# Two recurrent chains merged into one: both batches in one 512-column product, the line and the bias written into PSUM before it

## The reference

```
def _conv1d(x, w, b):
    y = jax.lax.conv_general_dilated(x, w, window_strides=(1,), padding=[(2, 2)], dimension_numbers=('NCH', 'OIH', 'NCH'))
    return y + b[None, :, None]
...
def step(w, b):

    def f(carry, inp):
        nxt = inp + _conv1d(carry, w, b)
        return (nxt, nxt)
    return f
...
_, d_rest = jax.lax.scan(step(down_w, down_b), d0, xs[1:])
...
_, u_rest = jax.lax.scan(step(down_w, down_b), u0, seq)
...
_, r_rest = jax.lax.scan(step(right_w, right_b), r0, ws[1:])
...
_, l_rest = jax.lax.scan(step(left_w, left_b), l0, R[Ww - 2::-1])
...
x = x + _L1_conv_ref(_gn(x), L1_conv_down_w, L1_conv_down_b, L1_conv_right_w, L1_conv_right_b, L1_conv_left_w, L1_conv_left_b)
```

## Time and profile before

| | |
|---|---|
| device time, median of 3 runs | 10,235.59 us (10,228.61 to 10,245.71) |
| span of the profiled execution | 10,244.7 us |
| recurrences, first to last product's start | 5097.5 to 9501.8 us |
| TensorE busy | 9248.3 us, 90% |
| VectorE busy | 7669.6 us, 75% |
| ScalarE busy | 6283.6 us, 61% |
| GpSimd busy | 2991.7 us, 29% |

### The profile page before, as it was taken

One profiled execution on the slowest core, in us unless ns is written; L12 is line 12 of the kernel. 1 busy time (PEld: TensorE's weight loads), 2 busy tenths in 40 slices (PEclk: granted clock), 3 DMA queues, 4 the chain that ended last, 5 costly groups with the idle time before them and its releaser, 6 DMA issues. The chain is left out here.

```text
span 10244.7 us, 212155 instructions
## 1 busy us (share of the span) xinstructions
PE 9248.3 (90%) x72264; PEld 8910.2 (87%) x72264; DVE 7669.6 (75%) x15539; ACT 6283.6 (61%) x11050; POOL 2991.7 (29%) x4335
## 2 busy tenths in 40 slices
PE   3999999999999999999899999999999999999100
PEld 3999999999999997777699999999999999999100
DVE  8888888777777775666677777777899987777323
ACT  3777777777777775444466668999633346666000
POOL 0000000000000000000166666666666666666000
PEclk9999999999999999999899999999999999999555
DMA  8888887666666666999889896777766657777999
GB/s 269 168 170 168 168 170 143 131 129 133 136 131 135 135 131 150 291 278 293 235 191 195 203 195 191 219 210 217 210 205 217 211 184 200 196 203 188 370 433 401
DMA packets 770603, 2101.31 MB, mean 205 GB/s; under 512 B 58976, under 2 KB 633728, under 8 KB 674256
## 3 DMA queue, kind: packets, MB, share of 16 engines
q1 hardware_dynamic: 629824, 1744.21, 66.6%
q0 software_dynamic: 34304, 151.01, 5.7%
q10 hardware_dynamic: 106368, 204.76, 5.6%
HBM read 1344.55 MB, written 754.97 MB: 205 GB/s over the span
## 5 line engine op out<-in xcount | busy, mean ns | idle before, releaser
L1542 ACT CAST hi<-rough 112x256 fp32r<-112x256 f32 x4096 | 1666.2, 407 | 1414.4 <-DVE rough L1455 1362.8
L1375 PE MATMUL scan_ps<-hi,scan_high 112*112 112x256 f32 x12264 | 2122.7, 282 | 30.7 <-ACT hi L1542 30.7
L1455 DVE SCALAR_TENSOR_TENSOR rough<-scan_ps,scan_bias,lines 112x256 f32<-112x256 f32 x4086 | 2136.4, 523 | 18.4 <-issue 14.0
L1386 PE MATMUL scan_ps_low<-lo,scan_high 112*112 112x256 f32 x12264 | 2136.1, 283 | 0.9 <-POOL lo L1487 0.7
L1381 PE MATMUL scan_ps_low<-hi,scan_low 112*112 112x256 f32 x12264 | 2123.9, 282 | 0.0
L463 PE MATMUL conv_ps<-tap_low,x_high 128*128 128x432 f32 (+2 forms) x6144 | 1905.4, 310 | 0.0
L463 PE MATMUL conv_ps<-tap_high,x_low 128*128 128x432 f32 (+2 forms) x6144 | 1904.0, 310 | 0.0
L463 PE MATMUL conv_ps<-tap_high,x_high 128*128 128x432 f32 (+2 forms) x6144 | 1882.0, 306 | 11.7 <-DVE x_edge L659 7.3
L1375 PEld LDWEIGHTS scan_ps<-hi,scan_high 112*112 112x112 f32 x12264 | 1695.0, 176 | 32.0 <-ACT hi L1542 31.5
L1386 PEld LDWEIGHTS scan_ps_low<-lo,scan_high 112*112 112x112 f32 x12264 | 1685.7, 176 | 6.3 <-POOL lo L1487 2.1
L1381 PEld LDWEIGHTS scan_ps_low<-hi,scan_low 112*112 112x112 f32 x12264 | 1684.1, 176 | 0.0
(11 more groups left out here) (142 smaller groups left out, 11625.5 us busy)
## 6 DMA issues: line engine op xcount, KB each, us to landing
raw<-x SPq DMA_DIRECT2D x764, 256.0 KB, 5.0
d_rows<-lines SPq DMA_DIRECT2D x32, 3584.0 KB, 30.4
u_cols<-lines SPq DMA_DIRECT2D x64, 1792.0 KB, 13.3
r_cols<-lines SPq DMA_DIRECT2D x32, 3584.0 KB, 24.3
lines<-u_cols SPq DMA_DIRECT2D x31, 3584.0 KB, 16.5
lines<-r_cols SPq DMA_DIRECT2D x30, 3584.0 KB, 16.6
lines<-d_rows SPq DMA_DIRECT2D x30, 3360.0 KB, 15.7
v_blocks<-xs ACTq DMA_DIRECT2D x128, 768.0 KB, 4.5
```

The source lines that it names most:

```text
L1375: last = nc.tensor.matmul(ps[:, b, 0:LP], high[:, shift], hi[:, b, (k - 1) % 2, shift:shift + LP], start=shift == 0, stop=shift == 2)
L1386: last = nc.tensor.matmul(ps_low[:, b, 0:LP], high[:, shift], lo[:, b, shift:shift + LP], start=False, stop=shift == 2)
L1455: nc.vector.scalar_tensor_tensor(rough[:, b, k % 2], ps[:, b, 0:LP], bias, line(way, s, k % T, b, kept), ALU.add, ALU.add).then_inc(rough_ ...
L1542: nc.scalar.copy(hi[:, b, k % 2, 1:LP + 1], rough[:, b, k % 2]).then_inc(hi_ready[b], 1)
```

## The change

Both batches of a line now share every instruction: products are 512 columns wide (two batches of 256), with one set of semaphores. PSUM holds four slots of 512 columns (`SLOTS`), and all nine products of a line add up in one of them. Before the first of them, VectorE writes the input line and the bias into the slot (`seed`); in "down" it writes scale and shift of the normalising in the same pass, one instruction for each batch, and ScalarE's normalising is gone. ScalarE reads `hi` from the slot after the three high products; when the six low products are in too, VectorE subtracts `hi` from the slot, which gives `lo`; the state is `hi` + `lo`, by GpSimd. `hi` has four buffers and `lo` two. ScalarE's turning copies run two lines later (`LAG`). SyncE's loads and stores wait on `seeded` and `state_done` in place of the per-batch semaphores. At the start four products set up the slots.

```diff
+    LAG = 2
+    AHEAD = 2
+    HIS, LOS, SLOTS = 4, 2, 4
...
-            return ctx.enter_context(nc.psum_tensor(name, [PP, B, 512], F32))
+            return ctx.enter_context(nc.psum_tensor(name, [PP, SLOTS, B, LP], F32))
...
-        rough = sb("rough", [PP, B, 2, LP])
-        hi = sb("hi", [PP, B, 2, LP + 2], F32R)
-        lo = sb("lo", [PP, B, LP + 2], F32R)
+        hi = sb("hi", [PP, HIS, B, LP + 2], F32R)
+        lo = sb("lo", [PP, LOS, B, LP + 2], F32R)
...
+        def slot_free(engine, way, g, k, kept):
+
+            if not (way == "down" and kept and k < SLOTS):
+                engine.wait_ge(lo_ready, states0(way) + T * g + k - SLOTS + 1)
+
+        def high_free(engine, way, g, k, first):
+
+            if not (way == "down" and first and k < HIS):
+                engine.wait_ge(state_done, states0(way) + T * g + k - HIS + 1)
...
-                def steps(way, g, start):
-                    high, low = w_hi[:, TAPS_OF[way]], w_lo[:, TAPS_OF[way]]
-                    done = states0(way) + T * g
-                    for k in range(start, 2 * T):
-                        for b in range(B):
-
-                            pe.wait_ge(hi_ready[b], done + k)
-                            for shift in range(3):
-                                last = nc.tensor.matmul(ps[:, b, 0:LP], high[:, shift], hi[:, b, (k - 1) % 2, shift:shift + LP],
-                                                        start=shift == 0, stop=shift == 2)
-                            last.then_inc(conv_done[b], 1)
-
-                            pe.wait_ge(state_done[b], done + k)
-                            for shift in range(3):
-                                nc.tensor.matmul(ps_low[:, b, 0:LP], low[:, shift], hi[:, b, (k - 1) % 2, shift:shift + LP],
-                                                 start=shift == 0, stop=False)
-
-                            pe.wait_ge(lo_ready[b], done + k)
-                            for shift in range(3):
-                                last = nc.tensor.matmul(ps_low[:, b, 0:LP], high[:, shift], lo[:, b, shift:shift + LP],
-                                                        start=False, stop=shift == 2)
-                            last.then_inc(low_done[b], 1)
+                def slot(k):
+                    return ps[:, k % SLOTS]
+
+                def high_products(way, g, k):
+
+                    pe.wait_ge(seeded[way], T * g + k + 1)
+                    pe.wait_ge(hi_ready, states0(way) + T * g + k)
+                    for shift in range(3):
+                        last = nc.tensor.matmul(slot(k), w_hi[:, TAPS_OF[way], shift], hi[:, (k - 1) % HIS, :, shift:shift + LP],
+                                                start=False, stop=False, skip_group_check=True)
+                    last.then_inc(conv_done, 1)
+
+                def low_products(way, g, k):
+
+                    pe.wait_ge(hi_ready, states0(way) + T * g + k + 1)
+                    for shift in range(3):
+                        nc.tensor.matmul(slot(k), w_lo[:, TAPS_OF[way], shift], hi[:, (k - 1) % HIS, :, shift:shift + LP],
+                                         start=False, stop=False, skip_group_check=True)
+
+                    pe.wait_ge(lo_ready, states0(way) + T * g + k)
+                    for shift in range(3):
+                        last = nc.tensor.matmul(slot(k), w_hi[:, TAPS_OF[way], shift], lo[:, (k - 1) % LOS, :, shift:shift + LP],
+                                                start=False, stop=shift == 2, skip_group_check=True)
+                    last.then_inc(low_done, 1)
+
+                def steps(way, g, first=False, last=False):
+                    for k in range(2 * T):
+                        if not (last and k == 2 * T - 1):
+                            high_products(way, g, k + 1)
+                        if not (first and k == 0):
+                            low_products(way, g, k)
 
...
+                for j in range(SLOTS):
+
+                    nc.tensor.matmul(slot(j), w_hi[:, 0, 0], hi[:, 0, :, 0:LP], start=True, stop=False, skip_group_check=True
+                                     ).then_inc(slots_set, 1)
                 for way in WAYS:
-                    steps(way, 0, 1)
-                    with pe.Fori(1, G // 2) as i:
-                        steps(way, 2 * i, 0)
+                    steps(way, 0, first=True)
+                    with pe.Fori(1, G // 2 - 1) as i:
+                        steps(way, 2 * i)
+                    steps(way, G - 2, last=True)
...
+                def seed(way, g, s, k, kept=False, bare=False):
+
+                    arrived(v, way, g, s, k % T, kept)
+                    slot_free(v, way, g - s, k, kept)
+                    to, of = ps[:, k % SLOTS], line(way, s, k % T, kept)
                     if way == "down":
-                        if k % 2 == 0:
-                            v.wait_ge(normed, T * g + k + 2)
-                    elif kept and KEPT[way][s]:
-                        if way == "up" and s == 1 and k == T - 1:
-                            v.wait_ge(skipped_in, 16)
-                    elif k == 0:
-                        v.wait_ge(loaded[way][s], landed(way, g, s))
-
+                        shift = gn1_bias if bare else down_shift
+                        for b in range(B):
+                            ins = nc.vector.tensor_scalar(to[:, b], of[:, b], gn1_scale[:, b:b + 1], shift[:, b:b + 1], ALU.mult, ALU.add)
+                    elif bare:
+                        ins = nc.vector.tensor_copy(to, of)
+                    else:
+                        ins = nc.vector.tensor_scalar(to, of, b_sb[:, TAPS_OF[way]:TAPS_OF[way] + 1], None, ALU.add)
+                    ins.then_inc(seeded[way], 1)
+
+                def steps(way, g, first=False, last=False):
+                    for k in range(2 * T):
+                        done = states0(way) + T * g + k
+                        v.wait_ge(hi_ready, done + 1)
+                        if not (first and k == 0):
+                            v.wait_ge(low_done, convs0(way) + T * g + k)
+                        if not (way == "down" and first and k < LOS):
+                            v.wait_ge(state_done, done - LOS + 1)
+                        nc.vector.tensor_tensor(low_of(k), ps[:, k % SLOTS], high_of(k), ALU.subtract).then_inc(lo_ready, 1)
+                        ahead = k + AHEAD
+                        if ahead < 2 * T:
+                            seed(way, g + ahead // T, ahead // T, ahead, first)
+                        elif not last:
+                            seed(way, g + ahead // T, ahead // T - 2, ahead - 2 * T)
+
...
-                            v.wait_ge(conv_done[b], convs + k)
-                            nc.vector.scalar_tensor_tensor(rough[:, b, k % 2], ps[:, b, 0:LP], bias, line(way, s, k % T, b, kept),
-                                                           ALU.add, ALU.add).then_inc(rough_ready[b], 1)
-
-                            v.wait_ge(low_done[b], convs + k)
-                            v.wait_ge(rough_ready[b], done + k + 1)
-                            nc.vector.tensor_tensor(state(way, s, k, b), ps_low[:, b, 0:LP], rough[:, b, k % 2],
-                                                    ALU.add).then_inc(state_done[b], 1)
...
+                        pool.wait_ge(hi_ready, states0(way) + T * g + k + 1)
+                        pool.wait_ge(lo_ready, states0(way) + T * g + k + 1)
+                        nc.gpsimd.tensor_tensor(state(way, s, k), high_of(k), low_of(k), ALU.add).then_inc(state_done, 1)
...
-                            nc.scalar.copy(hi[:, b, k % 2, 1:LP + 1], rough[:, b, k % 2]).then_inc(hi_ready[b], 1)
...
-                        if way == "down":
-                            ahead = k - k % 2 + LEAD
-                            if ahead < 2 * T or not last:
-                                s = (ahead // T) % 2
-                                group = g + ahead // T
-                                if ahead % T == 0 and k % 2 == 0:
-                                    act.wait_ge(loaded[way][s], landed(way, group, s))
-                                normalise(s, ahead % T, 2, k % 2).then_inc(normed, 1)
+                        if first and k == 0:
+                            act.wait_ge(seeded[way], 1)
+                        else:
+                            act.wait_ge(conv_done, convs0(way) + T * g + k)
+                        high_free(act, way, g, k, first)
+                        nc.scalar.copy(high_of(k), ps[:, k % SLOTS]).then_inc(hi_ready, 1)
+                        if way in laid:
+                            if not (first and k < LEAD + LAG):
+                                behind(way, g, k)
```

More of the change, by code:

```diff
@@ new lines, in _ @@
+                v.wait_ge(slots_set, SLOTS)
+                v.wait_ge(scale_ready, 1)
+                for way in WAYS:
+                    if way in laid:
+                        v.wait_ge(state_done, states0(way))
+                    elif way == "right":
```

(11 more changed lines are left out.)

130 lines of the change are left out of this document (47 added, 83 removed).

## The result

| | before | after |
|---|---|---|
| median of four runs, us | 10,237.1 | 16,491.3 |
| lowest to highest, us | 10,228.6 to 10,245.7 | 16,489.8 to 16,496.5 |
| span of the profiled execution, us | 10,244.7 | 16,490.9 |
| recurrences, us | 4404 | 10,654 |

The changed kernel is slower by a factor of 1.611 (95% interval 1.6087 to 1.6132), 6,254 us. It lies above the predicted range, in the stretch that the rival "the clock falls" had marked out, between 13,770 and 17,560.

A forecast was written before the change was run, and what follows sets the result against it. TensorE's stream of products was taken to bound the kernel. One serial chain of 3.76 us a line ("down" 3.89, "right" 4.10), 512 lines each, made 7941 us instead of 4404, +3537, so 13,770 us; range 12,950 to 14,700.

The forecast's parts named there:

- the clock falls: Rival: in the recurrences TensorE's waits keep its clock at 0.50, 17,560 us in all; low or swinging, chance 0.11.
- The mechanism: Recurrences: merged batches leave one serial chain, TensorE waiting on lo and seed some 1.5 us a line; +3537 us.
- the choice that the clock stays at 1.00: Recurrences: TensorE keeps its full clock despite the waits in each line, giving 13,770 us; chance 0.82.
- link 5: Way back from VectorE's seed to TensorE: 0.04 us hand-over plus 0.10 first weights, together 0.14 us a line.
- 1 and 2: Nine products of 512 columns, 2.07 us a line, then the last product's tail and VectorE's start, 0.19 us.
- 3: lo to the seed's start: VectorE's subtraction of 512 columns from PSUM and SBUF, until the seed starts: 0.61 us a line.
- 4: seed: VectorE's write of 512 columns into PSUM: 0.75 us a line, 0.88 in "down", 1.09 in "right".
- link 1: TensorE's nine products of 512 columns in a line, 0.23 us each: 2.07 us, bounds 1.92 to 2.15.
- the rival with two elements a cycle: Rival: VectorE's seed takes 0.49 us, a line 3.50 us, 13,240 us in all; inside the forecast's range, no separate chance.
- The cast and the addition: ScalarE's cast of hi (0.81 us) and GpSimd's addition (1.38 us) lie beside the chain and cost nothing.
- TensorE stays full: Rival: lo and seed are hidden beside another line's products, 2.07 us a line, 10,062 us in all; chance 0.05.

The follow-up runs named there:

- three added products: Changed kernel plus three 512-column products nobody reads, ahead of each line's high products: 14,136.81 us (one run).
- with both doubled: Changed kernel with six added unread products, plus ScalarE's cast and GpSimd's addition made twice in every line: 14,161.99 us.
- the two kernels that make it so: Changed kernel with seeds three lines ahead instead of two, 10,196.55 us; changed kernel with the seed issued before lo's subtraction, 10,197.68 us.
- the kernel with the seed twice: Changed kernel with six added unread products, plus every seed first written into an unread PSUM tile: 15,795.78 us.

## Why the prediction was wrong, point by point

**The mechanism was right.** One chain through TensorE and VectorE replaced two that covered each other; TensorE's wait is put down to the seed's line, as was written, and lo starts 0.09 us after the last low product ends (the profile names no releaser for that wait of VectorE). Cutting the chain at one place takes all of the loss away, and an addition to it is paid in full.

**The step that failed is the choice that the clock stays at 1.00**, put at 0.82 against 0.11. It rested on 3944 to 3952, in which TensorE was busy 5.06 of 8 us and granted 1.00. That row was read as a busy share, and the share is close to that of the changed kernel. But the timeline of the kernel before has one pause there, of 1.51 us, and products without a gap ahead of it.

```profile
3946.51 0.29 PE L469 MATMUL conv_ps<-edge_low,x_edge 128*128 128x288 f32 x1
3948.31 1.60 PE L444 MATMUL gram_ps<-xs 128*96 128x96 f32 x16 [1.51 <-DVE vt L671]
```

The changed kernel has a pause in each line, and nearly all are longer: 1.58 us in the loops of "up" and "left", 1.74 in "down", 1.83 to 1.90 in "right". There the clock was 0.59 to 0.69. Where the pause was 1.50 us, outside the loop of "up", the forecast's choice held: 1.00, and 3.88 us a line. The forecast's own links made a pause of 1.43 us in "up" and "left" (0.03 + 0.61 + 0.75 + 0.04), 1.56 in "down" and 1.77 in "right", so for "down" and "right" it had no row of a pause that long; and in "up" and "left" the hand-over in the loop, 0.13 us where link 5 had 0.04, made the pause 1.58 instead of 1.50. That so small a difference should matter could not be read from any row of before. What came about lies between the two cases: the clock neither stayed low (17,560) nor stayed full. The section of the Trainium skill that spoke for the rival ("A second HAM failure mode: psum-queue depth-cycling" in TensorE: Matmul & The Clock Gate) has the right outcome, a swing between both levels with short pauses between groups of products. The cycling through banks, after which it is named, is not what matters in the runs here: with four slots in turn and no pause, or a shorter one, the granted clock was 1.00.

**The links**, at the full clock in "up" with three added products, from the rows above:

| link | predicted, us | measured, us |
|---|---|---|
| 1 and 2: nine products, first weights, tail, start of lo | 2.07 + 0.10 + 0.19 | 2.45 (7999.22 to 8001.67) |
| 3: lo to the seed's start | 0.61 | 0.61 |
| 4: seed | 0.75 | 0.74 |
| 5: to TensorE, without the weights | 0.04 | 0.14 (8003.02 to 8003.16) |
| a line | 3.76 | 3.94 |

Of the 0.18 us, 0.10 are the way back from VectorE to TensorE, for which the way to ScalarE was taken; in the loops of "up", "right" and "left" it is 0.13 to 0.14, in "down" and outside the loops 0.05 to 0.06. The other 0.09 lie in link 1 (0.03, a product being 0.2333 us) and in VectorE's start, 0.09 us after the last product's end (8000.71 + 0.87 to 8001.67) instead of 0.03. In "down" the two seeds took 0.98 instead of 0.88, and a line is 4.11 instead of 3.89; in "right" it is 4.26 instead of 4.10. With these lines the prediction's sum would have been 8,300 - 4404 + 10,236 = 14,132, and the kernel with three added products, from which they come, took 14,137: nothing outside the lines is missing. So the forecast was 2.6% short in its sizes, and 2,354 us short for the clock.

**The seed's price** was right: 744 ns for 512 columns from contiguous lines, with the median at 744 to 746 in all runs with seeds of 512, where the rival with two elements a cycle had 0.49 us. The rule of the Trainium skill on the page VectorE: DVE Perf Modes, "The perf-mode tier table", that a PSUM operand takes fp32 to one element a cycle, agrees with this for a write into PSUM too.

**The cast and the addition**, put at nothing, were nothing: with both doubled, 5 us.

**A slip of reading** changed no number: in the earlier trace rows the clock is 8 tenths in the twentieth slice, where the recurrences begin, and falls in the last three slices, not four.

**"TensorE stays full"** was worked out at 10,062 and needed the seed to be there before L(k-1) ends. The order ruled it out, as was said; the two kernels that make it so took 10,197.

## What to carry to other kernels

When two independent chains are merged into larger instructions, ask what the engine at the bound now does while the others work on its result; the count of instructions doesn't tell it. An instruction that is needed early, and depends on nothing late, must not stand behind a wait in its engine's queue: here moving it ahead of one subtraction took the kernel from 16,491 to 10,198 us, 0.4% under the kernel before. And where a change puts a pause into every step, price it at the low TensorE clock too: a stretch with one pause is no evidence for longer ones in every step, and here 1.50 us a line kept the clock where 1.58 didn't. Products that nobody reads are a quick way to split a loss into pauses and clock.

## What the runs showed of the hardware

- The granted clock can go up and down again within a line of 5 us, and with pauses of 1.58 to 1.90 us in each line this was worth 2,354 us. With 1.50 us in each line of 3.88 us it stayed at 1.00 for 119 us, and with pauses cut to 0.86 us ("up") and 1.2 us ("right") by three added products it was 1.00 in every window.
- From the end of a seed on VectorE to TensorE's first product took 0.05 to 0.06 us outside the loops and 0.13 to 0.14 in the loops of "up", "right" and "left".
- A seed from strided lines into PSUM ("right") took 1.07 us for 512 columns (at 11409.46 in the changed kernel), 0.33 more than from contiguous ones, as the strided rows had it.
- Two VectorE instructions of 512 columns that follow each other start 0.60 to 0.66 us apart (9003.85, 9004.45 and 9005.11 in the kernel with the seed twice), though the second seed's own record is 0.74 us long: what a queue pays for an added instruction is the former, and a waiting engine sees the latter.
